# Patches by embedding group, text on another queue and in five parts: the start of a fused transformer kernel

## The reference

```python
x = jnp.einsum('bnf,df->bnd', patches(data), W_lin) + b_lin        # 32 x 36 x 768 -> 32 x 36 x 256
h = jnp.concatenate([cls, x], axis=1) + position_embeddings
h = jnp.concatenate([h, txt], axis=1)                               # 32 x 165 x 256
h = h + attention(layernorm(h))                                     # 16 heads, causal, masked columns
h = h + experts(layernorm(h))                                       # 8 experts, each takes its top 660 tokens
```

## Time and profile before

| | us |
|---|---|
| median of 3 runs | 857.08 (855.34 to 858.67) |
| the profiled execution | 859.55 |
| its span, first to last instruction | 857.7 |
| PE busy in the span | 744.2 (87%) |
| DVE, ACT, POOL busy | 573.1, 397.3, 374.7 |
| mean granted TensorE clock | 0.928 |

### The profile page before, as it was taken

One profiled execution on the slowest core, in us unless ns is written; L12 is line 12 of the kernel. 1 busy time (PEld: TensorE's weight loads), 2 busy tenths in 40 slices (PEclk: granted clock), 3 DMA queues, 4 the chain that ended last, 5 costly groups with the idle time before them and its releaser, 6 DMA issues. The chain is left out here.

```text
span 857.7 us, 18735 instructions
## 1 busy us (share of the span) xinstructions
PE 744.2 (87%) x6840; PEld 673.3 (78%) x6840; DVE 573.1 (67%) x1343; ACT 397.3 (46%) x857; POOL 374.7 (44%) x504
## 2 busy tenths in 40 slices
PE   3699999999999999999997511379999999999994
PEld 2577888888888888888885411369999999999994
DVE  1135777668768768667664378776787787887561
ACT  0214455454455455455443155035557366475570
POOL 3113464464465454465444223023537347355334
PEclk9899999999999999999998755569999999999998
DMA  8952675555774675475661342011344453442122
GB/s 273 307 96 48 89 117 97 86 104 98 108 119 99 94 99 96 103 119 99 96 90 51 94 149 74 29 28 43 72 132 64 117 144 49 127 102 32 34 32 32
DMA packets 80686, 82.36 MB, mean 96 GB/s; under 512 B 36161, under 2 KB 74943, under 8 KB 80244
## 3 DMA queue, kind: packets, MB, share of 16 engines
q1 hardware_dynamic: 67980, 66.92, 38.8%
q0 software_dynamic: 11584, 10.96, 8.2%
q10 hardware_dynamic: 1032, 3.30, 1.1%
HBM read 34.59 MB, written 16.22 MB: 59 GB/s over the span
## 5 line engine op out<-in xcount | busy, mean ns | idle before, releaser
L595 POOL DMA_INDIRECT out<-r_arena x48 | 80.3, 1674 | 118.2 <-DVE r_arena L1530 107.9
L656 ACT ACTIVATE r_arena<-ps_all 126x660 f32<-126x660 f32 x128 | 92.2, 720 | 56.9 <-PE ps_all L879 55.3
L1249 DVE RECIPROCAL r_arena<-ps_all 128x165 f32<-128x165 f32 x64 | 76.1, 1189 | 61.3 <-PE ps_all L894 61.3
L520 POOL TENSOR_SCALAR_AFFINE_SELECT r_arena<-r_arena 126x660 f32<-126x660 f32 x128 | 97.0, 767 | 45.9 <-ACT r_arena L656 45.5
L1238 DVE TENSOR_REDUCE mx<-ps_all 128x4 f32<-128x504 f32 (+1 forms) x160 | 105.0, 669 | 15.3 <-PE ps_all L856 13.8
L879 PE MATMUL ps_all<-Qp,Kp 98*126 98x166 f32 x512 | 84.6, 289 | 7.9 <-ACT r_arena L656 6.1
L856 PE MATMUL ps_all<-Kp,Qp 96*65 96x56 f32 (+1 forms) x512 | 90.6, 293 | 0.0
L1552 DVE TENSOR_TENSOR hT_lo<-r_arena,hT_hi 128x330 fp32r<-128x330 f32 x128 | 63.2, 502 | 39.8 <-ACT r_arena L760 39.6
L582 POOL DMA_INDIRECT xe<-xn_rows,r_arena x48 | 59.8, 1245 | 63.4 <-issue 36.5
L1111 PE MATMUL ps_all<-xeT_hi,W_hi 128*128 128x330 f32 x256 | 83.1, 325 | 1.1 <-DVE hT_lo L1552 1.1
L758 ACT ACTIVATE hT_hi<-ps_all,vec_s 128x330 fp32r<-128x330 f32 x128 | 68.9, 539 | 32.4 <-PE ps_all L1111 30.1
(11 more groups left out here) (178 smaller groups left out, 1706.6 us busy)
## 6 DMA issues: line engine op xcount, KB each, us to landing
H<-w SPq DMA_DIRECT2D x16, 1024.0 KB, 5.6
Qp<-q_hi SPq DMA_DIRECT2D x64, 166.0 KB, 3.9
Kp<-k_hi SPq DMA_DIRECT2D x128, 63.0 KB, 4.1
Qp<-q_lo SPq DMA_DIRECT2D x32, 166.0 KB, 4.7
out<-H SPq DMA_DIRECT2D x16, 330.0 KB
xn_rows<-r_arena SPq DMA_DIRECT2D x16, 330.0 KB
Kp<-k_lo SPq DMA_DIRECT2D x64, 63.0 KB, 4.1
H<-h SPq DMA_DIRECT2D x1, 3360.0 KB, 22.6
```

What stands on the lines that cost most here:

```text
L520: pool.affine_select(PT[0:S, g, :, :], PT[0:S, g, :, :], [[0, 4], [STEP - 1, T]], ALU.is_ge, 0.0, base=STEP - 2, channel_multiplier=-STEP) ...
L595: pool.indirect_dma_start(rows_out, bass.IndirectOffsetOnAxis(tok[0:A, e % NTB, a:a + 1], 0), yw[0:A, a, :], None, bounds_check=NTOK - 1, ...
L656: act.activation(PT[0:S, g, :, :].rearrange("p (k h) t -> p k h t", k=2), pair[:, :, :, 0:T], ACT.Exp, scale=float(HD) ** -0.5).then_inc(e ...
L1249: dve.reciprocal(rS[:, c, :], bank(2 + c)[:, T:2 * T]).then_inc(rs_sum, 1)
```

## The change

1. The patches are laid out by embedding group, in HBM (last line of the diff) and in SBUF: what a group needs is one run per partition. `XP` has four loads: group 0, groups 1 to 3, groups 4 to 6, groups 7 to 10. SP issues the first three at once, the fourth after the first two moves.
2. The text is issued by ACT and cut in five: pair 0 behind the class rows, pairs 1 and 2 behind the broadcast rows, pairs 3 to 5 at the end of the loads, pairs 6 to 10 at the start of round 0, pairs 11 to 15 at the start of round 6. The class rows are placed per part, so there are five placements instead of three; those of the last two parts are in rounds 3 and 13 on SP.
3. On PE the embedding groups 0 to 5 run in a row, group 6 behind the first transposes, 7 to 10 between the products of samples 0 and 1, and none is left behind the row maxima of sample 0. DVE's additions are moved to match.

```diff
-XP = ((0, 1), (1, 4), (4, NG))
-HP = ((0, 1), (1, 3), (3, 6), (6, NPAIR))
+XP = ((0, 1), (1, 4), (4, 7), (7, NG))
+HP = ((0, 1), (1, 3), (3, 6), (6, 11), (11, NPAIR))
...
 @block.sync
-            cols = [slice(a * GB * NP, min(B, z * GB) * NP) for a, z in XP]
+            cols = [slice(KF * a * GB * NP, KF * min(B, z * GB) * NP) for a, z in XP]
...
-            def place_cls(a, z, i):
+            def place_cls(i):
+                a, z = HP[i]
+                sp.wait_ge(h_in[i], 16)
                 sp.dma_start(H4[0:1, a:z, 0, :], cls_s[a:z, 0, :]).then_inc(cls_moved[i], 16)
                 sp.dma_start(H4[T - A:T - A + 1, a:z, 1, :], cls_s[a:z, 0, :]).then_inc(cls_moved[i], 16)
...
             load_x(0)
-            load_h(0)
             load_x(1)
+            load_x(2)
             sp.wait_ge(addend_ready, 2)
-            sp.wait_ge(h_in[0], 16)
-            place_cls(0, 1, 0)
+            place_cls(0)
             move_embedded(0)
             move_embedded(1)
-            load_h(1)
-            load_x(2)
-            load_h(2)
-            sp.wait_ge(h_in[1], 16)
-            place_cls(1, 3, 1)
+            load_x(3)
+            place_cls(1)
             move_embedded(2)
             move_embedded(3)
-            load_h(3)
...
+                if b == 3:
+                    place_cls(3)
+                if b == 13:
+                    place_cls(4)
...
 @block.scalar
+            load_h(0)
             act.dma_start(cf[:, :], const_f).then_inc(cf_in, 16)
             act.dma_start(W_s[:, :, :, :], watt).then_inc(w_in, 16)
...
+            load_h(1)
             act.dma_start(cb[:, :], const_b).then_inc(cb_in, 16)
+            load_h(2)
...
+                if b == 0:
+                    load_h(3)
+                if b == 6:
+                    load_h(4)
...
 @block.vector, round_of
+                if b == -4:
+                    for g in (1, 2, 3):
+                        embedded(g)
                 if u == 0 and n + 2 < NPAIR:
                     ln1_stats_of(n + 2)
...
+    x = np.concatenate([x[:, :, g * GB * NP:(g + 1) * GB * NP].reshape(128, -1) for g in range(NG)], axis=1)
```

More of the change, by code:

```diff
@@ L192, in build @@
         at[0] = 0
-        xT_s = cut(R_ARENA, KF, B * NP)
+        xT_s = cut(R_ARENA, KF * B * NP)
         wl_s = cut(R_ARENA, KF, D)
@@ L268, in v_rows @@
             return V[:, i].rearrange("p w x -> p (w x)")[:, w * 272 - 16 * w + j * 32:w * 272 - 16 * w + j * 32 + 32]
-        x_in = [sem(f"x_in{i}") for i in range(3)]
-        h_in = [sem(f"h_in{i}") for i in range(4)]
+        x_in = [sem(f"x_in{i}") for i in range(4)]
+        h_in = [sem(f"h_in{i}") for i in range(5)]
         wl_in, add_in, cf_in, cb_in, w_in, vec_in, row_in = [sem(n) for n in (
@@ L275, in build @@
         addend_ready = sem("addend_ready")
-        cls_moved = [sem(f"cls_moved{i}") for i in range(3)]
+        cls_moved = [sem(f"cls_moved{i}") for i in range(5)]
         moved = [sem(f"moved{i}") for i in range(NPAIR)]
@@ L330, in _ @@
         def _(sp):
-            cols = [slice(a * GB * NP, min(B, z * GB) * NP) for a, z in XP]
+            cols = [slice(KF * a * GB * NP, KF * min(B, z * GB) * NP) for a, z in XP]
             def load_x(i):
-                sp.dma_start(xT_s[:, :, cols[i]], xT[:, :, cols[i]]).then_inc(x_in[i], 16)
-            def load_h(i):
+                sp.dma_start(xT_s[:, cols[i]], xT[:, cols[i]]).then_inc(x_in[i], 16)
+            def place_cls(i):
                 a, z = HP[i]
-                sp.dma_start(H4[0:HROWS, a:z], h0[:, a * RT:z * RT, :].rearrange("p (n r) d -> p n r d", r=RT))\
-                  .then_inc(h_in[i], 16)
-            def place_cls(a, z, i):
+                sp.wait_ge(h_in[i], 16)
                 sp.dma_start(H4[0:1, a:z, 0, :], cls_s[a:z, 0, :]).then_inc(cls_moved[i], 16)
@@ L405, in _ @@
                     move_embedded(5)
-                    sp.wait_ge(h_in[2], 16)
-                    sp.wait_ge(h_in[3], 16)
-                    place_cls(3, NPAIR, 2)
+                    place_cls(2)
                     move_embedded(6)
                     move_embedded(7)
+                if b == 3:
+                    place_cls(3)
+                if b == 13:
+                    place_cls(4)
                 if 0 <= b < B - 8:
@@ L612, in _, with load_h @@
             act.dma_start(cls_s[:, :, :], clsrows).then_inc(add_in, 16)
+            def load_h(i):
+                a, z = HP[i]
+                act.dma_start(H4[0:HROWS, a:z], h0[:, a * RT:z * RT, :].rearrange("p (n r) d -> p n r d", r=RT))\
+                   .then_inc(h_in[i], 16)
+            load_h(0)
             act.dma_start(cf[:, :], const_f).then_inc(cf_in, 16)
@@ L796, in embed @@
                 for k in range(KF):
-                    mm = pe.matmul(bank(g % 4)[0:n, 0:D], xT_s[:, k, g * GB * NP:g * GB * NP + n], wl_s[:, k, :],
+                    mm = pe.matmul(bank(g % 4)[0:n, 0:D], xT_s[:, KF * g * GB * NP + k * n:KF * g * GB * NP + (k + 1) * n], wl_s[:, k, :],
                                    start=(k == 0), stop=(k == KF - 1))
@@ L946, in early_rounds @@
             def early_rounds():
-                for g in range(3):
+                for g in range(6):
                     embed(g)
@@ L951, in early_rounds @@
                 transposes1(0, 1, None)
+                embed(6)
                 pe.wait_ge(w_in, 16)
@@ L954, in early_rounds @@
                 queries(0, query_bank(-2))
-                embed(3)
                 keys(0, key_bank(-2))
+                embed(7)
                 values(0)
+                embed(8)
                 queries(1, query_bank(-1))
                 keys(1, key_bank(-1))
-                embed(4)
+                embed(9)
                 values(1)
                 bias_through()
-                for g in (5, 6, 7):
-                    embed(g)
+                embed(10)
                 pe.wait_ge(cb_in, 16)
@@ L974, in early_rounds @@
                 max_transposes(0)
-                for g in (8, 9, 10):
-                    embed(g)
             def round_of(b):
@@ L1193, in ln1_stats_of @@
             def ln1_stats_of(n):
-                if n in (0, 1, 3):
-                    dve.wait_ge(cls_moved[min(n, 2)], 32)
+                for i, (first, _) in enumerate(HP):
+                    if n == first:
+                        dve.wait_ge(cls_moved[i], 32)
                 dve.wait_ge(moved[n], 32)
@@ L1270, in round_of @@
                 if b == -4:
-                    for g in (1, 2):
+                    for g in (4, 5):
                         embedded(g)
@@ L1277, in round_of @@
                     ins.then_inc(bvB_ready, 1)
+                    embedded(6)
                 if b == -1:
+                    for g in (7, 8):
+                        embedded(g)
                     low_q(1)
                     low_k(1)
-                    embedded(4)
+                    embedded(9)
                     dve.wait_ge(bpe_done, 1)
@@ L1284, in round_of @@
                     dve.tensor_tensor(bpe[0:A, :], bank(5)[0:A, 0:D], bp_s[0:A, :], ALU.add).then_inc(bpe_ready, 1)
-                    for g in (5, 6, 7):
-                        embedded(g)
+                    embedded(10)
                 if has_r:
@@ L1290, in round_of @@
                     low_q(b + 2)
-                if b == -2:
-                    embedded(3)
                 if has_r:
@@ L1303, in round_of @@
                     copy_mT(b + 1)
-                if b == -1:
-                    for g in (8, 9, 10):
-                        embedded(g)
                 if u == 0 and has_p:
```

## The result

The changed kernel takes 865.55 us (median of 4 runs, 865.18 to 866.18) where the kernel before took 857.27 (median of 4 on the same chip, 855.34 to 858.67). The ratio is 1.0099, with a 95% interval of 1.0078 to 1.012: it is slower by 1%, where 1.2% faster was forecast. The profiled executions have spans of 864.0 and 857.7 us.

What follows compares the result with a forecast made beforehand. TensorE, busy 87% of the span, was the engine to watch, with savable waits in the start. Gains of 18.2 less 2.5, 2.0, 1.5, 1.0 and 0.6 gave 10.6 us: 846.5 from the 857.08 median, range 841 to 854.

Steps and rivals of the forecast that it cites:

- First start: Start, wait for the first patches: first matmul at 6.6 us in place of 9.74, 3.1 us gained (0 to 4.2).
- Second load: Start, second load of patches: its 3.42 us wait and 1.5 us of half clock go, 4.9 us gained (0 to 4.9).
- Pair 1: Start, ahead of the first values product: the 5.25 us wait and 3.6 of slow clock go, 8.9 gained (0 to 8.9).
- Small waits: Start, waits of 0.88 and 1.41 us go, less 1.0 for pair 0's statistics and transposes: 1.3 us gained.
- The cover: Round 0, without the last three embedding groups key scores wait for the row maxima: 2.5 us lost (1.6 to 3.5).
- The load in round 0: Round 0, text of pairs 6 to 10 issued just ahead of the maxima's DMA: 2.0 us lost (0 to 5.0).
- Clock: Round 0, half clock behind TensorE's wait of about 4.5 us: 1.5 us lost (0 to 3.6).
- The load in round 6: Round 6, text of pairs 11 to 15 in front of the maxima: 1.0 us lost (0 to 4.1).
- Class placements: Rounds 3 and 13, two SyncE issues each ahead of the maxima: 0.6 us lost in all (0 to 2.5).
- rival in which the maxima wait for each whole load: Rounds 0 and 6: losses of 5.0, 3.6 of slow clock and 4.1 leave 2.4 gained, 854.7 us; chance 0.10.
- slower rival: Rounds 0 and 6: each load takes 11.3 us with 3.6 of slow clock, 13.8 us more, 870.9; chance 0.04.

Runs made afterwards that it cites:

- layout-only run: The kernel before with the patches laid out by embedding group and nothing else; 857.92 us, ratio 0.9985.
- moves-alone run: The changed kernel with ACT issuing the text of pairs 1 to 5 only once pair 0's patch rows are in H; 859.4 us, ratio 1.0023.
- the five short ones: The changed kernel with each of the two text loads of the rounds issued as five DMAs of one pair, same moment; 862.32 us, ratio 1.006.
- a pair a round: The changed kernel with the text of pairs 6 to 15 issued one pair per round in rounds 0 to 9, behind the first exponentials; 851.17 us, ratio 0.9901.
- text in the start: The changed kernel with both text loads of the rounds issued behind the third text load of the start, none in the rounds; 860.18 us, ratio 1.0008.
- text issued behind the scores: The changed kernel with the same two text loads issued one step later on ACT, behind the first exponentials of rounds 0 and 6; 858.47 us, ratio 0.9999.

## Why the prediction was wrong

Its reading of the start and of what a missing cover does held; the sizes of two terms and one left out turned the sign.

- *First start*: 6.6 expected, 6.43 measured. *Second load*: no wait, six groups by 24.2 us (24.8). *Pair 1*: the wait and its half clock are gone. The first two terms, 8.0 us, came in full. The third, 8.9, may have had some luck: PE came late to the values product because of pair 0. In the two runs that mend this the statistics of pair 1 are waited for again, 1.2 and 1.8 us ahead of that product; but they issue its text later too, so they don't tell whether it would have been in time. In the layout-only run the second load lands 6.5 us sooner (11.6 in place of 18.2); about 4.1 of these it has from the text of pair 0 ahead of it, which lands sooner too, and some 2.4 are its own, so here the 1296-byte pieces were slower than 7776-byte ones (an estimate from the landings of two runs).
- *Small waits*: this is the first step that failed, a wait put at nothing. I let the statistics of pair 0 follow DVE's addition at 19.9 and took the landing of its patch rows for granted. The moves had been used 3.6 us after their issue; now they and the class rows ahead of them stood beside ACT's queue with weights, constants and all the text of the start, and it took 9.8 us, to 25.3: 5.9 us more of wait than the 1.0 allowed and 1.8 of slow clock (transposes 1.33, group 3.83 us). The moves-alone run gives 25.32 for the transposes, against the 25.8 of the prediction, and round 0 comes 6.0 us sooner.
- *The cover*: 2.5 expected, 1.6 measured where no load is beside it. SyncE was not late.
- *The load in round 0*: this is the second step that failed, 2.0 expected of 0 to 5.0, 5.6 measured (8.2 us from the queries to the key scores, 2.6 without the load). Two parts of this were wrong. The load does not last 5.0 us: I took 346 GB/s from a stretch of patches, and it needs 9.4 us from issue to landing, at 271 GB/s. And I read the earlier trace rows as "small pieces get through", from a stretch in which the small pieces were the long queue; I also left out the patch-row move that stands ahead of the maxima on SP's queue. *Clock*: 1.5 expected, 3.0 measured.
- *The load in round 6*: 1.0 expected, 7.9 measured, 5.4 of waiting and 2.5 of clock, for which I had allowed no clock at all.
- *Class placements*: 0.6 for both expected, about 0.6 for each measured; they are seen in rounds 4 and 14 of every run that has them in rounds 3 and 13.

The rival in which the maxima wait for each whole load (854.7) had a chance of 0.10. The trace agrees with it in part: from 58 to 61 us not one piece of SP's queue moved, and from 61 to 64 us 36 rows went beside 50 pieces of text, about one row to a piece (an estimate from these counts). But the maxima did not only wait for the load: the 36 rows ahead of them on their own queue went at the pace of the text first. The rival had the waits in the rounds nearly right (5.0 and 4.1; 5.6 and 5.4 measured); it lacked the clock behind round 6's wait and the late moves of the start. The slower rival named the right cause, the two loads with their slow clock, at a chance of 0.04; its price of 11.3 us a load was above the measured 5.6 and 5.4, and its break-even of 4.4 us of stall a load was passed by both. With the start as predicted that would still have been close to even: the kernel with the moves alone, its two waits in the rounds unchanged, stands at 1.0023. Together with the late moves it made the sign.

What stays open is why nothing of SP's queue moves for the first 3 us beside such a load, and 1 us beside the five short ones; no run tells whether the number of pieces, their bytes or the ends of DMAs set it. That each of the three stalls came with ACT's queue full (107.8% from 15 to 18 us, 90.8% from 58 to 61, 103.2% from 142 to 146), and went when the text was held back (moves alone), cut and issued one part at a time behind the maxima (a pair a round) or, for those of the rounds, taken away (text in the start), is shown.

## What to carry to other kernels

A small DMA on which an engine waits should not be issued beside a long load of another queue (in round 0 TensorE started 7.7 us after the issue of the maxima, where it was 2.14 without the load): before moving a load "to where the DMA engines are idle", list the small transfers of that stretch, who waits for each and with how much to spare. If the load must be there, cut it into parts that are issued one at a time, behind the waited-for transfer; here that turned +1.0% into -1.0%, and with the start mended into -1.7%. And price a wait of TensorE with the slow clock behind it, at every place where it may occur.

## What the runs showed of the hardware

- Two hardware queues did not share the DMA engines evenly over 3 us: SP's DMAs, issued at 57.86 us (maxima) and 64.1 us (packing, with text issued behind the scores), moved nothing in 58 to 61 and 65 to 69 us, while 53 and 70 pieces of 15360 bytes went by.
- Once both queues moved, the small one went at the pace of the large one: 36 rows of 1 KB beside 50 pieces of text from 61 to 64 us, where the move before had its 36 rows through in under 1 us. With all text in the start it was 32 rows beside 62 pieces from 38 to 42 us.
- The text loads, with 112 runs of 15360 bytes, moved 269 to 271 GB/s, less than the 341 GB/s of patches, weights and text together from 10 to 20 us. No run shows why.
- Each of the three waits of TensorE of 6.9, 6.8 and 5.1 us was followed by work at half the clock (granted 0.50 from 27.6 to 34.4 us, from 65.5 to 72 and from 148.5 to 152), which cost 1.8, 3.0 and 2.5 us on top of the wait. In the kernel before it was 0.50 from 18.1 to 20.0 us, behind the wait of 3.42 us, and from 36.5 to 44.0, behind the one of 5.25.
